# Attention B: scores and mixes of two pairs in one burst, softmax six pairs ahead

## The reference, cut to what matters

```python
q = rope(einsum('bim,mhd->bhid', x, wq))      # 16 heads of 128
k = rope(einsum('bim,mhd->bhid', x, wk))
v = einsum('bim,mhd->bhid', x, wv)
s = einsum('bhid,bhjd->bhij', q * mult, k * mult)
s = s - 1e30 * mask                           # j > i is masked
p = softmax(s)
o = einsum('bhij,bhjd->bhid', p, v)
r = einsum('bhid,hdm->bim', o, wo)            # x = x + r
```

## Time and profile before

| | before |
|---|---|
| median of 3 runs | 1534.94 us |
| the profiled execution: time, span | 1532.65 us, 1530.8 us |
| busy share PE, DVE, ACT, POOL | 95%, 77%, 55%, 40% |
| mean granted TensorE clock | 0.988 |
| attention B in the trace | some 690 to 1245 us |

### The profile page before, as it was taken

How to read it: one execution, slowest core, us unless ns; L and a number is a source line. 1 busy time by engine, 2 the same in 40 slices (tenths; PEclk the granted TensorE clock), 3 DMA queues, 4 the chain that set the end, 5 groups by cost and what they waited for, 6 DMA issues and landing times. The chain is left out here.

```text
span 1530.8 us, 26737 instructions
## 1 busy us (share of the span) xinstructions
PE 1460.8 (95%) x8904; PEld 1262.2 (82%) x8904; DVE 1171.8 (77%) x2661; ACT 835.6 (55%) x2040; POOL 612.7 (40%) x484
## 2 busy tenths in 40 slices
PE   8799999997899999988999999999999879999998
PEld 6677777776788888876899999999999868888887
DVE  7899999998765555587888888888888777555554
ACT  4788888885433333227766666666666433333322
POOL 2587777874100000017766656666666210000000
PEclk9899999999999999999999999999999999999999
DMA  2265555555210000003223223213222200010001
GB/s 101 55 162 145 148 148 149 155 129 141 84 42 21 22 21 0 1 4 98 52 70 69 63 63 69 70 43 86 67 49 52 53 22 22 21 42 21 0 0 56
DMA packets 73156, 100.17 MB, mean 65 GB/s; under 512 B 10304, under 2 KB 63552, under 8 KB 73024
## 3 DMA queue, kind: packets, MB, share of 16 engines
q1 hardware_dynamic: 73024, 98.55, 24.5%
HBM read 37.56 MB, written 2.23 MB: 26 GB/s over the span
## 5 line engine op out<-in xcount | busy, mean ns | idle before, releaser
L1840 DVE TENSOR_TENSOR f_hidden<-ps,f_silu 128x512 f32<-128x512 f32 x128 | 87.7, 690 | 201.5 <-PE ps L122 201.5
L482 POOL TENSOR_TENSOR ab_swapped<-ab_swapped,const 128x512 f32<-128x512 f32 x126 | 162.9, 1293 | 166.9 <-ACT ab_swapped L477 166.1
L1731 ACT ACTIVATE f_silu<-ps 128x512 f32<-128x512 f32 x128 | 76.3, 598 | 276.2 <-PE ps L122 276.2
L120 PE MATMUL ps<-xh,f_wl 128*128 128x512 f32 x512 | 203.2, 397 | 1.6 <-DVE f_hidden L1840 1.6
L121 PE MATMUL ps<-xl,f_wh 128*128 128x512 f32 x512 | 202.8, 396 | 0.0
L122 PE MATMUL ps<-xh,f_wh 128*128 128x512 f32 x512 | 202.5, 396 | 0.0
L1543 POOL TENSOR_TENSOR ab_qk<-ab_qk,ab_swapped 128x512 f32<-128x512 f32 x126 | 172.5, 1369 | 9.9
L1311 ACT ACTIVATE ab_probs<-ab_probs,ab_negmax 128x128 f32<-128x128 f32 (+1 forms) x256 | 114.6, 449 | 81.9 <-DVE ab_negmax L1414 77.5
L73 POOL TENSOR_TENSOR rstd<-shifted,minus_half 128x4 f32<-128x4 f32 x16 | 16.2, 1013 | 339.6 <-DVE shifted L67 339.6
L120 PE MATMUL ps<-f_wh,f_hl 128*128 128x256 f32 x512 | 144.2, 282 | 0.4 <-DVE x L1856 0.4
L121 PE MATMUL ps<-f_wl,f_hh 128*128 128x256 f32 x512 | 143.9, 281 | 0.0
(11 more groups left out here) (210 smaller groups left out, 4377.8 us busy)
## 6 DMA issues: line engine op xcount, KB each, us to landing
ab_probsT<-ab_squares SPq DMA_DIRECT2D x128, 192.0 KB, 3.6
aa_probsT<-f_stages SPq DMA_DIRECT2D x128, 128.0 KB, 2.6
b_stages<-keys SPq DMA_DIRECT2D x128, 128.0 KB, 2.8
f_stages<-wf_in SPq DMA_DIRECT2D x16, 768.0 KB, 4.4
aa_spread<-inv_rows SPq DMA_DIRECT2D x64, 128.0 KB, 3.0
b_stages<-wb_qkv_in SPq DMA_DIRECT2D x8, 768.0 KB, 6.4
a_stage<-wa_in SPq DMA_DIRECT2D x8, 608.0 KB, 4.3
x<-x_in SPq DMA_DIRECT2D x4, 512.0 KB, 7.2
```

Of the source, the lines that this page charges most:

```text
L120: nc.tensor.matmul(out, ll, rh, start=start, stop=False)
L482: return engine.tensor_tensor(by_batch(out), by_batch(src), table(c, rows, col), ALU.mult)
L1840: nc.vector.tensor_tensor(hidden[:, m, :], UP(m), silu[:, m, :], ALU.mult).then_inc(hid_done, 1)
```

## The change

LEAD goes from 7 to 6. PE makes scores and mixes only in steps 0 and 2, and then of two pairs: the scores of the pairs 6 and 7 ahead, then the mixes of the pairs 2 and 1 behind. So the burst of step 1 moves into step 2 and the burst of step 3 into the next slot's step 0. DVE and ACT still take one pair in each step, now the one 6 ahead. The prologue makes one pair less ahead, and one mix more stands at the end.

```diff
-    W, SQ, LEAD = T + P, 32, 7
+    W, SQ, LEAD = T + P, 32, 6
...
             def step(it, half, s, j):
                 first, last = is_first(it), is_last(it)
-                if exists(it, s, j, LEAD):
-                    scores(*moved(it, s, j, LEAD))
-                if not (first and s == 0 and j == 0):
-                    mix(*moved(it, s, j, -1))
+                if j % 2 == 0:
+                    for by in (LEAD, LEAD + 1):
+                        if exists(it, s, j, by):
+                            scores(*moved(it, s, j, by))
+                    for by in (-2, -1):
+                        if not (first and s == 0 and j == 0):
+                            mix(*moved(it, s, j, by))
...
             project_values(0, 0, 0, 1)
-            scores(0, 1, 2)
...
                 head_pair(it, it % 2)
+            mix(HP - 1, NG - 1, PAIRS - 2)
             mix(*LAST)
...
             take_values(0, 0, 1)
-            exps(0, 1, 2)
...
             row_max(0, 1, 1)
-            for j in range(2):
-                invert(0, 1, j)
-                turn_squares(0, 1, j)
-            row_max(0, 1, 2)
+            invert(0, 1, 0)
+            turn_squares(0, 1, 0)
```

## The result

The changed kernel takes 1566.18 us (median of five runs, 1565.21 to 1569.6), the one before 1534.85 (five runs). The ratio is 1.0208, 95% interval 1.019 to 1.0226: slower by 31.3 us. The profiled executions have spans of 1564.3 us after and 1530.8 before.

What follows compares the result with a forecast made beforehand. PE was taken to bound attention B's middle, with DVE only just in time in step 3 (margin 0.22 us). 33.6 − 0.3 − 1.9 + 0.1 = +31.5 us on 1534.94 gave 1566.4 us, range 1560 to 1573.

Steps and rivals of the forecast that it cites:

- The hole at output 2: Step 3, 28 slots: without the burst's cover, PE waits at output 2 for DVE's adds of output 1.
- The loss per slot: Burst moved out of step 3: 1.31 − 0.06 − 0.05 = 1.20 us in each of 28 slots, +33.6 us.
- the sign: PE's waits at output 2 for DVE's adds: some 28 of 1.1 to 1.2 us each, 31 to 34 us in total.
- The seams: 64 fewer changes between f32 burst and split matmuls in PE's queue: −0.3 us, bounds 0 and −5.4.
- Step 1's burst: Moved into step 2: output 0 stays where it was and DVE may start up to 0.67 us earlier; cost 0.
- the second scores: Second scores of a double burst wait for the odd step's row_max: margin 1.3 us in step 2, cost 0.
- output 3: In step 0 it waits for add 2; PE gets 1.31 us more ahead of it, DVE the same work: cost 0.
- Opening: Start of attention B: one pair less scored ahead, PE's DMA and POOL holes close: −1.9 us, bounds 0 and −2.5.
- Closing: Last head pair and end: POOL hole goes, −0.75 us; one more mix, +0.85; together +0.1, bounds −1 and +1.5.
- The sum: 33.6 − 0.3 − 1.9 + 0.1 = +31.5 us on the median of 1534.94: 1566.4 us.
- second wait per slot: Rival: the double burst meets maxed or mix_lo late, 1.1 us a slot, 31 us more: 1597; chance 5%.
- the clock rival: Regular holes in the 28 slots lower TensorE's clock, 1.8 us each, 50 us: 1617; chance 3%.

Runs made afterwards that it cites:

- e2: Kernel before with DVE's and ACT's softmax six ahead and only step 3's burst moved, into the next slot's step 0: 1566.98 us (1.0219).
- e3: Changed kernel, but in step 3 DVE adds output 1 ahead of row_max, inversion and transpose: 1531.74 us (0.9989 of the kernel before).
- e5: Changed kernel, but PE makes output 2 in the next slot's step 0, behind the double burst, except in the last head pair: 1534.17 us (1.0001).
- e8: Changed kernel with one spare DVE transpose in step 3, between the pair's own transpose and the add: 1589.98 us (1.0370 of the kernel before).
- e9: Kernel before with one spare DVE transpose in step 3, between the pair's own transpose and the add: 1557.03 us (1.0158).
- e4: Kernel before with only DVE's and ACT's softmax ordered six ahead, PE's steps unchanged: 1530.58 us (0.9979).
- e1: Kernel before with DVE's and ACT's softmax six ahead and only step 1's burst moved, into step 2; PE's prologue and end unchanged: 1529.97 us (0.9979).
- e6: Changed kernel with one spare DVE sum of two SBUF tiles in step 3, between transpose and add: 1595.5 us (1.0409 of the kernel before).
- e7: Kernel before with one spare DVE sum of two SBUF tiles in step 3, between transpose and add: 1583.76 us (1.0328).

## Why the prediction was right

- *The hole at output 2.* As forecast: place, owner and count. Chain from L482 to the adds' end: 2.98 forecast, 902.91 + 0.96 − 900.89 = 2.98 measured. Second matmul of output 2 behind the adds' end: 0.28 and 904.15 − 903.87 = 0.28. Period 17.74 and 17.75. e2 has it alone; e3 and e5 remove it in two ways, e8 and e9 lengthen it.
- *The loss per slot.* 1.20 forecast, 34.44 / 28 = 1.23 measured, +34.4 us where I had 33.6. The 0.03 is of the size that merging costs (next item). The profile's bracket reads 0.93 a wait, not the 1.1 to 1.2 I had named as the sign: it counts from the modelled end. The 28 waits are 26.0 us of the 33.9, so that the total fell into my 31 to 34 us is not a confirmation.
- *The seams.* −0.3 us forecast, wrong in sign. From the first output 0 to the one 28 slots on, e4 takes 462.43 us and e1, with 28 merged pairs of bursts, 463.51; e3, with 56 and DVE's add moved, 463.22. So merging costs some 1 us and not less than nothing; it doesn't grow with the count, and where in the slot it lies stays open. The term of 0.005 us also hangs on rounding: at the spacings as they are given, four of 0.11 and four of 0.22, eight passes take 1.32 us, more than the burst's 1.31.
- *Step 1's burst, the second scores, output 3, ACT, SP: cost 0.* Right: e1 has no wait in the slots. In the changed kernel the margin of output 3 behind its add grew from 0.14 to 1.36 us in its tightest slots, and that of output 0 behind mixed_lo from 0.12 to 0.89. Both had been tighter than the 0.22 at output 2; they cost nothing because this change moves no work of PE from ahead of them to behind them.
- *Opening.* −1.9 forecast. From the scores that resume behind the wait for negmax (714.52 and 715.47) to the first output 0 (738.20 and 737.33) it is −1.82. The DMA and POOL holes of the earlier trace rows are gone. Ahead of that the clock was at its lower level for 6.8 us and not 3.4, and most of what that cost the shorter wait (0.34 and not 1.64) took back; the whole row is −1.50:

```profile
715.47 1.55 PE L1174 MATMUL ps<-ab_qk 128*128 128x128 f32 x8 [0.34 <-DVE ab_negmax L1416]
721.09 1.48 PE L1174 MATMUL ps<-ab_qk 128*128 128x128 f32 x8
722.40 0.59 PE L1192 MATMUL ps<-ab_probsT,ab_values 128*128 128x256 f32 x2
```

- *Closing.* +0.1 forecast, −1.36 measured. The POOL hole of the earlier trace rows went: up to the last output 2 it is −0.70, with −0.75 forecast. The mis-sized part is from there to the last mix, +0.85 forecast, where I kept the lower clock: before, output 2 and one mix took 2.72 us at it (1228.91 to 1231.63); after, output 2 and two mixes took 2.12 at the full one (1261.79 to 1263.91, first matmul 0.39 long, not 0.58), −0.60. The clock fell later, in the experts, for +1.32.

```profile
1261.79 0.39 PE L120 MATMUL ps<-b_woh,ab_ml 128*128 128x256 f32 x1 [1.88 <-DVE x L1440]
```

- *The sum, and luck in it.* The forecast is within 0.3 us of the median, 1566.4 and 1566.18, which is closer than its terms are. The spans of the two profiled executions differ by 33.5 us, 2.0 more than the 31.5 of the sum: +1.1 in the 28 slots (34.44 against 33.6 − 0.3), +0.6 ahead of the stage, +0.4 in the opening, −1.5 in the closing and +1.3 in the experts. The profiled execution before was 2.2 us below its median (1532.65 and 1534.85), the one after is the median itself, and the two differences cancel. What the runs bear out is the mechanism and its 34.4 us in the 28 slots.

- *The rivals.* No second wait per slot; the granted clock stayed at 1.00 through all 28 holes. The Trainium skill's rule on swings of the clock by short idling ("TensorE: Matmul & The Clock Gate", section "A second HAM failure mode: psum-queue depth-cycling") did not show with these holes of 0.93 us, one every 17.75.

What is not shown: that a second bank for the outputs would remove the hole too. All eight PSUM banks are in use, and it wasn't tried.

## What to carry to other kernels

An engine that is busy in 100% of a stretch can still owe that to another one that is just in time: before moving work inside its queue, list for each of its waits what stands between the event that starts the other engine's chain and the wait, and how long that chain is. Work moved from before such a wait to behind it is lost whole, less the margin, and of a margin of 0.22 us only 0.06 counted here. The cheap cure is on the other engine's side: the operation that is waited for goes first in its step (e3). With it the change comes out level with the kernel before (0.9989), and no more: merged bursts bring nothing. e1 and e4, which share the softmax's order, measured 0.2% below the kernel before (1529.97 and 1530.58 us); since the traces place only 0.7 us of e4's gain in or behind the stage, that the order is what earns it is not shown.

## What the runs showed of the hardware

*Two SBUF inputs beside POOL.* The spare sum of two SBUF tiles takes 0.65 us on DVE in 24 of e6's 28 slots and 1.70 to 1.78 in e7, with the same operands, and 0.65 to 0.69 in both where POOL is idle. What differs is when POOL's own operation started. In all 28 slots of e7 and in four of e6 it started 0.06 to 0.14 us ahead of DVE's; POOL's kept its length (1.26 to 1.30), and DVE's ended some 0.5 after it. In the other 24 slots of e6 the two starts lie within 0.02 of each other; there DVE's kept its length, and POOL's took 1.79:

```profile
894.44 1.79 POOL L1546 TENSOR_TENSOR ab_qk<-ab_qk,ab_swapped 128x512 f32<-128x512 f32 x1
894.45 0.65 DVE L1451 TENSOR_TENSOR ab_spare<-const 128x512 f32<-128x512 f32 x1
```

Each is longer by most of the other's length, so shifting POOL by less than a tenth of a microsecond moves 1.1 us onto DVE's chain. The spare transposes of e8 and e9 kept their length (0.83 to 0.87) at both kinds of start. The Trainium skill ("SBUF — State Buffer", section "Who interferes with whom") says that a DVE operation with two SBUF inputs contends with a GpSimd one that reads SBUF, and that the order of issue decides which of them is blocked. The trace agrees where POOL is 0.06 us or more ahead. In e6 POOL's record is the earlier by 0.01 to 0.02 in 22 of the 24 slots, and DVE's still went first; whether the records have the order of issue right at such a distance isn't shown.

*The clock behind a longer hole.* In four of e6's slots, the first three and the last, the spare operation was long, and PE's holes read 2.62 us. The first left the clock at 1.00. At the other three it went to its lower level (1.2 of 2.4 GHz), for 3.4, 6.8 and 3.4 us: 0.3 and 0.7 us ahead of the matmul that ended the second and the third hole, and 0.4 behind the one that ended the fourth. Windows of e6, the first over the second and the third hole, the second over the 24 slots with the short form, with the columns of the earlier trace rows:

```profile
742.00:803.00 61.00, 54.85 (x312) 49.05 (x312) 45.89 (x119) 32.23 (x84) 30.05 (x24) 0.92 0.22 54
803.00:1240.00 437.00, 400.40 (x2473) 359.71 (x2474) 355.31 (x947) 261.72 (x684) 264.09 (x191) 1.00 0.23 55
```

In the 28 slots, holes of 1.69 us in e8, of 1.54 in the rest of e6, of up to 1.41 in e7 and of 0.93 in the changed kernel left it at 1.00. In the last head pair, where PE waits more often, a hole of 1.86 to 1.90 us stands before the last output 2 in the two kernels and in e1 to e5. The clock was down at its end in the kernel before, e3 and e5, fell within 1.5 us behind it in e2 and e4, and did neither in the changed kernel and e1. So the clock rival has its mechanism in this kernel, and the runs show it in the middle of the stage at 2.62 us and not at the holes of this change.
